# The units of a state-space scan in another order, without the two spare products with zero in each

## The chip, the cores and the metric

The kernel runs on one NeuronCore of one Trainium2 chip. The metric is the device time of one launch in microseconds (us); a time is the median of the runs named beside it. The engines are called by the names of the profile: PE (TensorE; PEld are its weight loads), DVE (VectorE), ACT (ScalarE), POOL (GpSimd) and SP (SyncE, which only issues DMAs here).

## What is computed

A small network on an image of 2 x 16 x 16 positions with 64 channels: an edge attention, an attention with rotary positions, a second attention, a mixture of experts, six layers of a state-space model, and a second mixture of experts. The change is in the state-space layers only. For each of the six layers and both batches (256 positions, 128 inner channels, 16 states):

```python
residual = hidden + residual
hidden = rmsnorm(residual, norm_w[i])
u, z = split(hidden @ in_w)                       # 128 channels each
uc = silu(causal_conv(u, cw) + cb)                # four taps
dt_r, Bm, Cm = split(uc @ xp_w)                   # 16 columns each
dt = softplus(dt_r @ dt_w + dt_b)
A = -exp(A_log)
h = exp(dt[..., None] * A) * h + (dt * u)[..., None] * Bm[:, None, :]   # along the positions
y = einsum('bds,bs->bd', h, Cm) + uc * D
hidden = (y * silu(z)) @ out_w
```

## The kernel before

The state-space layers run as 12 **units**, one for each layer and batch, `u = 0..11` with batch `b = u % 2`. In a unit the inner channels lie on the 128 partitions and the positions along the free axis. The 16 states are four **groups** `g` of four states `s`, so one operation of a group works on 128 x 1024 values. The order of work on each engine is written out by hand; engines wait for each other by semaphores, and each engine takes its instructions in the order in which they stand.

In a unit the work goes like this:

- ACT makes the decay factors, `decay` (L1487): one exponential of 128 x 255 for each state, 16 in a unit, four to a group.
- `drive` makes dt·u·B for a group: DVE for groups 0 and 1 (L1173), from rows of B that PE spreads over the partitions (`replicate`, L661, four small products; `spread_first`, `spread_second`), POOL for groups 2 and 3 (L1691), from rows that a DMA has spread.
- DVE scans each group along the positions (`scan`, L1182).
- `weigh` multiplies the states by C: POOL for groups 0 to 2 (L1702), the third in two halves; DVE for group 3 (`weigh_last`, L1192, two halves) from rows that PE spreads (`spread_last`).
- PE adds the 16 products up in PSUM by products with the identity (`sum_y` L694, `sum_third` L700, `sum_last` L708) on top of the product with D (`sum_skip`, L686).
- DVE multiplies the sum by silu(z) (`gate`, L1166), PE projects it and adds the residual (`out_proj`, L717 and L720).

Beside the scans of unit u, the next unit u+1 is prepared, and its input is the residual that unit u-1 of the same batch has just left: the squares (`prep_norm`, ACT, L1417), the root on POOL (`prep_rms`, L1674 and L1676), the scaled rows (`prep_hs`, ACT, L1431), turned by PE (`prep_transpose`, L622 to L626), copied (`prep_ht`, ACT, L1437), the convolution and the products for z (`prep_in`, PE, L633 to L637), tanh (`prep_tu`, ACT, L1443), `prep_uc` (DVE, L1148), `prep_x` (PE, L644 to L646: dt, B and C), the copies of B and C (`prep_xd`, ACT, L1461 and L1462), two steps that split them into three bf16 parts (`take_away` on PE, L653, and `prep_part` on ACT, L1467), the softplus (`prep_softplus`, ACT, L1471 to L1477), and `prep_dt` (DVE, L1154 to L1160).

Two products with a weight of zero, `idle_turns(2)` (L726), stand on PE between `sum_skip` and `prep_transpose` in each unit but the last; they add nothing to the sum. On PE a unit stands like this before the change:

```python
if u:
    sum_last(u - 1)
    sum_third(u - 1, 1).then_inc(sem("m_y"), 1)
    out_proj(u - 1)
spread_second(u); sum_skip(u); idle_turns(2); prep_transpose(u + 1); spread_last(u)
prep_in(u + 1); prep_x(u + 1); sum_y(u, 0); take_away(u + 1, 0)
sum_y(u, 1); take_away(u + 1, 1); sum_third(u, 0); spread_first(u + 1)
```

The functions that the change touches, with the line numbers of the profile:

Of the kernel before, what the change touches and what calls it, by code (L numbers as in the profile page):

```python
# [29 lines left out]
SG = 4  # L30
NSG = DS // SG
UNITS = NL * B
# [35 lines left out]
def hybrid(nc, x, const, w0, w1, w2, w3, w5, wm, rows, out):  # L68
    ctx = ExitStack()
    with ctx:  # L70
# [7 lines left out]
        def sem(name):  # L78
            if name not in sems:
                sems[name] = ctx.enter_context(nc.semaphore(name))  # L80
            return sems[name]
# [25 lines left out]
        ident = CONST.of(cst, "ident")  # L107
# [170 lines left out]
        def _(pe):  # L278
# [350 lines left out]
            def prep_in(u):  # L629

                i, b = divmod(u, 2)
                pe.wait_ge(sem("m_ht"), u + 1)
                pe.matmul(ups, bias[:, :, 0], pick_b[:, i:i + 1].to_broadcast([96, N]), start=True, stop=False)  # L633
                pe.matmul(ups, wcv[:, i, 0], ht[b][:, 3:3 + N], start=False, stop=False)
                pe.matmul(ups, wcv[:, i, 1], ht[b][:, 1:1 + N], start=False, stop=True).then_inc(sem("m_in"), 1)

                pe.matmul(zps, inz[:, i], ht[b][0:64, 3:3 + N], start=(u == 0), stop=True, skip_group_check=True)\  # L637
                    .then_inc(sem("m_in"), 1)

# [31 lines left out]
            def spread_second(u):  # L671

                pe.wait_ge(sem("m_dbu"), 2 * u + 1)
                replicate(u, SG)
# [10 lines left out]
                pe.wait_ge(sem("m_zs"), u + 1)  # L685
                pe.matmul(yps, dmat[:, i], uc[b], start=True, stop=True)  # L686

            def sum_y(u, g, zs_of=None):

                pe.wait_ge(sem("m_hc"), 4 * u + g + 1)  # L690
                if zs_of is not None:
                    pe.wait_ge(sem("m_zs"), zs_of + 1)
                for s in range(SG):
                    pe.matmul(yps, ident, hc[:, g, s], start=False, stop=True, skip_group_check=True)  # L694

            def sum_third(u, h):

                pe.wait_ge(sem("m_hc"), 4 * u + 3 + h)
                for s in range(2 * h, 2 * h + 2):
                    last = pe.matmul(yps, ident, hc[:, 2, s], start=False, stop=True, skip_group_check=True)  # L700
                return last

            def sum_last(u):

                for h in range(2):
                    pe.wait_ge(sem("m_hc3"), 2 * u + h + 1)
                    for s in range(2 * h, 2 * h + 2):
                        pe.matmul(yps, ident, hc[:, NSG - 1, s], start=False, stop=True, skip_group_check=True)  # L708

            def out_proj(u):  # L710

# [17 lines left out]
            def keep_awake(count, bank=5):  # L729

                for _ in range(count):
                    pe.matmul(PS[:, bank, N:2 * N], ident, CONST.of(cst, "rope")[:, 0:N], start=True, stop=True)  # L732
# [4 lines left out]
            keep_awake(1)  # L737
            pe.wait_ge(sem("m_weights"), 5)
            prep_in(0)
            keep_awake(3)  # L740
            prep_x(0)
            take_away(0, 0)
# [4 lines left out]
            for u in range(UNITS):  # L747
                more = u + 1 < UNITS
                if u:
                    sum_last(u - 1)  # L750
                    sum_third(u - 1, 1).then_inc(sem("m_y"), 1)
                    out_proj(u - 1)
                spread_second(u)
                sum_skip(u)
                if more:
                    idle_turns(2)
                    prep_transpose(u + 1)
                spread_last(u)
                if more:
                    prep_in(u + 1)  # L760
                    prep_x(u + 1)
                sum_y(u, 0, u + 1 if more else None)
                if more:
                    take_away(u + 1, 0)
                sum_y(u, 1)
                if more:
                    take_away(u + 1, 1)
                sum_third(u, 0)
                if more:
                    spread_first(u + 1)  # L770
            sum_last(UNITS - 1)
            sum_third(UNITS - 1, 1).then_inc(sem("m_y"), 1)
            out_proj(UNITS - 1)
            spare(1, 5)

# [38 lines left out]
        def _(v):  # L814
# [361 lines left out]
            def scan(u, g):  # L1176

                v.wait_ge(sem("m_dbu" if g < 2 else "m_dbu_pool"), 2 * u + g % 2 + 1)
                v.wait_ge(sem("m_da"), u * NSG + g + 1)
                if u and g < NSG - 1:  # L1180
                    v.wait_ge(sem("m_hc"), 4 * (u - 1) + (g + 1 if g < 2 else 4))
                v.tensor_tensor_scan(flat(hst[:, g]), flat(da[g % 2]), flat(dbu[:, g]),  # L1182
                                     0.0, ALU.mult, ALU.add).then_inc(sem("m_h"), 1)

# [109 lines left out]
        def _(act):  # L1294
# [174 lines left out]
            def prep_softplus(u):  # L1469

                act.activation(sp_a, dtp, ACT.Abs).then_inc(sem("m_sp"), 1)  # L1471
                act.wait_ge(sem("m_sp"), 4 * u + 1)
                act.activation(sp_v, sp_a, ACT.Tanh, scale=LOG_K, bias=turn_t).then_inc(sem("m_sp"), 1)
                act.activation(sp_u, sp_a, ACT.Exp, scale=-1.0, bias=logs_t).then_inc(sem("m_sp"), 1)
                prep_part(u, 1)
                act.wait_ge(sem("m_sp"), 4 * u + 2)
                act.activation(sp_w, sp_v, ACT.Tanh, scale=LOG_M, bias=shift_t).then_inc(sem("m_sp"), 1)  # L1477

# [25 lines left out]
            for u in range(UNITS):  # L1504
                more = u + 1 < UNITS
                decay(u, 0, every)
                decay(u, 1, every[0:3])
                if u:
                    act.wait_ge(sem("m_hid"), u)
                if u and more:  # L1510
                    prep_norm(u + 1)
                if u:
                    keep_residual(u - 1)
                decay(u, 1, every[3:4])
                if u and more:
                    prep_hs(u + 1)
                decay(u, 2, every[0:1])
                if more:
                    prep_ht(u + 1)
                decay(u, 2, every[1:3])  # L1520
                if more:
                    prep_tu(u + 1)
                decay(u, 2, every[3:4])
                if more:
                    prep_zs(u + 1)
                decay(u, 3, every[0:2])
                if more:
                    prep_xd(u + 1)
                decay(u, 3, every[2:4])
                if more:  # L1530
                    prep_softplus(u + 1)
                    prep_z(u + 1)
                    prep_part(u + 1, 2)
# [32 lines left out]
        def _(pool):  # L1566
# [140 lines left out]
            for u in range(UNITS):  # L1707
                more = u + 1 < UNITS
                drive(u, 2)
                if u and more:  # L1710
                    prep_rms(u + 1)
                weigh(u, 0)
                drive(u, 3)
                weigh(u, 1)
                weigh(u, 2, 2)
                if more:
                    prep_gz(u + 1)
# [101 lines left out]
```

## Time and profile before

| what | value |
|---|---|
| median of 3 runs | 383.85 us (383.53 to 384.74) |
| the profiled execution, its own time | 383.59 us |
| span of the profiled execution | 381.8 us |
| mean granted clock of PE over the span | 0.939 of full speed |
| PE busy | 329.2 us (86%) |
| DVE busy | 285.5 us (75%) |
| ACT busy | 236.2 us (62%) |
| POOL busy | 195.9 us (51%) |
| the 12 units | from about 158 to 357 us of the span |

A row of the timeline gives start, duration, engine, line, operation, what is written from what, and in square brackets how long the engine had been idle before it and what ended that. A row of the chain gives start, duration and name of one piece of the chain of work that ended last. A row of the windows gives a stretch, its length, the busy time of PE, PEld, DVE, ACT and POOL in it with the number of instructions, the granted clock of PE (1.00 is 2.4 GHz, 0.50 is 1.2 GHz) and the DMA share.

### The profile page before, as it was taken

How to read it: one execution, taken by the hardware profiler on the slowest of the kernel's cores; microseconds unless marked ns; L12 is line 12 of the kernel's file. 1: busy time of each engine (PE TensorE's matmuls, PEld its weight loads, DVE VectorE, ACT ScalarE, POOL GpSimd, SP SyncE). 2: the span in 40 equal slices, each digit the busy share in tenths (PEclk: the TensorE clock that was granted, in tenths of full speed). 3: DMA queues.
4: the chain of work that ended last, by engine and by line, in shares of the span. 5: the costliest groups of instructions: out<-in, count | busy, mean ns of one | idle time of the engine just before them, and what ended most of it. 6: DMA issues, size and time to landing. Idle time of an engine off the chain costs nothing.

```text
span 381.8 us, 5717 instructions
## 1 busy us (share of the span) xinstructions
PE 329.2 (86%) x1904; PEld 233.6 (61%) x1904; DVE 285.5 (75%) x496; ACT 236.2 (62%) x674; POOL 195.9 (51%) x175
## 2 busy tenths in 40 slices
PE   4866998899989999689989889898898989878684
PEld 3354875556548547466667666676766767656562
DVE  2674477989764543599998989889898998988363
ACT  1103278887870664786877867777686877863163
POOL 2989200000000410397887968888696887967000
PEclk9995699999996899999999999999999999995968
DMA  7960400000000030635427163461725527160000
GB/s 212 364 119 3 124 2 1 2 2 1 3 0 2 5 108 0 212 127 218 169 110 274 33 250 113 164 231 51 278 67 211 162 116 278 34 245 0 1 2 14
DMA packets 19751, 41.07 MB, mean 108 GB/s; under 512 B 7986, under 2 KB 10626, under 8 KB 19594
## 3 DMA queue, kind: packets, MB, share of 16 engines
q1 hardware_dynamic: 19434, 40.38, 31.0%
q8 instruction: 15, 0.25, 0.3%
q10 hardware_dynamic: 288, 0.33, 0.3%
q14 instruction: 14, 0.11, 0.1%
HBM read 40.31 MB, written 0.39 MB: 107 GB/s over the span
## 4 chain that ended last, share of the span: by engine, by line
PE 52%; DVE 28%; ACT 9%; issue 6%; POOL 3%; DMA 1%; DVEq 0%; SPq 0%; POOLq 0%; ACTq 0%
DVE big L1182 14%; PE PS L708 5%; PE PS L521 4%; DVE big L1192 3%; PE PS L661 3%; PE PS L700 3%; PE PS L297 2%; PE PS L485 2%; ACT PS L1487 2%; PE PS L415 2%; PE PS L732 2%; PE PS L585 2%; PE PS L291 2%; PE PS L495 2%; PE PS L622 2%
## 5 line engine op out<-in xcount | busy, mean ns | idle before, releaser
L1182 DVE TENSOR_TENSOR_SCAN big<-PS,big 128x1024 f32<-128x1024 f32 x48 | 109.6, 2287 | 5.6 <-ACT PS L1487 5.2
L1487 ACT ACTIVATE PS<-unit_t,amat 128x255 f32<-128x255 f32 x192 | 82.5, 467 | 20.7 <-DVE unit_t L1157 16.6
L1702 POOL TENSOR_TENSOR big<-big 128x1024 f32<-128x1024 f32 (+1 forms) x48 | 86.2, 1821 | 3.1 <-DVE big L1182 2.4
L1691 POOL TENSOR_TENSOR big<-unit_t,big 128x1024 f32<-128x1024 f32 x24 | 57.1, 2381 | 17.9 <-DMA big<-spill 17.9
L694 PE MATMUL PS<-big,cst 128*128 128x256 f32 x192 | 50.1, 407 | 1.3 <-POOL big L1702 1.2
L1658 POOL TENSOR_TENSOR w2t<-w2t,w0t 128x768 f32<-128x768 f32 x2 | 3.6, 1821 | 88.8 <-DVE big L1116 88.8
L694 PEld LDWEIGHTS PS<-big,cst 128*128 128x128 f32 x192 | 37.6, 201 | 8.1 <-POOL big L1702 2.6
L1298 ACT ACTIVATE big<-PS 128x512 f32<-128x512 f32 (+1 forms) x43 | 24.7, 583 | 22.5 <-PE PS L521 7.4
L1350 ACT ACTIVATE big<-PS,big 128x256 f32<-128x256 f32 x64 | 29.7, 474 | 1.5 <-DVE big L956 1.4
L1173 DVE TENSOR_TENSOR big<-unit_t,PS 128x1024 f32<-128x1024 f32 x24 | 29.0, 1208 | 1.7 <-PE PS L661 0.6
L661 PE MATMUL PS<-stack,pick_b 96*128 96x256 bf16 x144 | 22.2, 277 | 7.5 <-DVE big L1173 4.0
L956 DVE TENSOR_REDUCE big<-PS 128x2 f32<-128x512 f32 x32 | 22.0, 688 | 6.3 <-PE PS L485 3.0
L700 PE MATMUL PS<-big,cst 128*128 128x256 f32 x96 | 24.8, 380 | 0.0
L521 PE MATMUL PS<-cst,big 128*128 128x128 f32 x128 | 20.9, 285 | 3.2 <-ACT big L1298 1.9
L708 PE MATMUL PS<-big,cst 128*128 128x256 f32 x96 | 22.7, 379 | 0.0
L521 PEld LDWEIGHTS PS<-cst,big 128*128 128x128 f32 x128 | 13.5, 140 | 14.4 <-DVE big L965 6.9
L661 PEld LDWEIGHTS PS<-stack,pick_b 96*128 96x128 bf16 x144 | 12.5, 102 | 15.4 <-ACT stack L1467 7.6
L965 DVE TENSOR_SCALAR big<-big 128x256 f32<-128x256 f32 x64 | 19.7, 351 | 1.1
L700 PEld LDWEIGHTS PS<-big,cst 128*128 128x128 f32 x96 | 17.7, 193 | 3.1
L708 PEld LDWEIGHTS PS<-big,cst 128*128 128x128 f32 x96 | 17.3, 190 | 2.1
L1674 POOL TENSOR_TENSOR msq<-ssq,eps_t 128x2 f32<-128x2 f32 x11 | 2.2, 197 | 29.3 <-ACT sqs L1417 29.3
L1192 DVE TENSOR_TENSOR big<-big,PS 128x512 f32<-128x512 f32 x24 | 15.4, 684 | 0.4
(336 smaller groups left out, 663.2 us busy)
## 6 DMA issues: line engine op xcount, KB each, us to landing
big<-spill SPq DMA_DIRECT2D x60, 512.0 KB, 5.9
w3t<-in_w SPq DMA_DIRECT2D x1, 1588.0 KB, 13.6
big<-routed SPq DMA_DIRECT2D x8, 128.0 KB, 2.9
w2t<-in_w SPq DMA_DIRECT2D x1, 896.0 KB, 9.8
cst<-in_const SPq DMA_DIRECT2D x1, 848.0 KB, 7.7
w5t<-in_w SPq DMA_DIRECT2D x1, 812.0 KB, 6.0
w2t<-in_wm SPq DMA_DIRECT2D x1, 768.0 KB, 4.7
w1t<-in_w SPq DMA_DIRECT2D x1, 385.0 KB, 8.2
```

What stands on the lines that cost most here:

```text
L521: last = pe.transpose(PS[:, 6 + t, m * N + a * P:m * N + (a + 1) * P], probs[:, i % SLOTS, a, m * P:(m + 1) * P], ident)
L661: last = pe.matmul(PS[:, 4 + c, s * N:(s + 1) * N], pick_b[:, col:col + 1].to_broadcast([96, P]), stack[u % 2][:], start=True, stop=True)
L694: pe.matmul(yps, ident, hc[:, g, s], start=False, stop=True, skip_group_check=True)
L700: last = pe.matmul(yps, ident, hc[:, 2, s], start=False, stop=True, skip_group_check=True)
L708: pe.matmul(yps, ident, hc[:, NSG - 1, s], start=False, stop=True, skip_group_check=True)
L1173: v.tensor_tensor(dbu[:, g], dtu[u % 2].unsqueeze(1).to_broadcast([P, SG, N]), BCv, ALU.mult)\
L1182: v.tensor_tensor_scan(flat(hst[:, g]), flat(da[g % 2]), flat(dbu[:, g]), 0.0, ALU.mult, ALU.add).then_inc(sem("m_h"), 1)
L1192: v.tensor_tensor(hc[:, g, s], hst[:, g, s], BCv[:, s], ALU.mult).then_inc(sem("m_hc3"), 1)
L1350: act.activation(probs[:, i % SLOTS, a], PS[:, i % 4, a * N:(a + 1) * N], ACT.Exp, bias=rowmax[:, i, a:a + 1], accum_out=rowsum[:, i, a:a ...
L1487: one = act.activation(da[g % 2][:, n, 1:N], dt[u % 2][:, 1:N], ACT.Exp, scale=amat[:, u // 2, col:col + 1])
L1691: pool.tensor_tensor(dbu[:, g], dtu[b].unsqueeze(1).to_broadcast([P, SG, N]), bsp[b][:, SG * (g - 2):SG * (g - 1)], ALU.mult).then_inc(sem ...
L1702: pool.tensor_tensor(hc[:, g, s:s + size], hst[:, g, s:s + size], csp[u % 2][:, SG * g + s:SG * g + s + size], ALU.mult).then_inc(sem("m_h ...
```

## The change

Within each unit the order on PE, ACT and POOL changes, and the products with zero are no longer issued (the function stays, nothing calls it). No operation is added; `weigh` for groups 0 and 1 is cut into two halves like that for group 2, and each sum on PE waits for the half that it reads. `prep_in` is cut in two, so that the product for z stands behind `spread_last`.

```diff
+            def prep_in_z(u):
+
+                i, b = divmod(u, 2)
                 pe.matmul(zps, inz[:, i], ht[b][0:64, 3:3 + N], start=(u == 0), stop=True, skip_group_check=True)\
...
+            def sum_y(u, g, some):
+
+                for s in some:
+                    if g < NSG - 1:
+                        pe.wait_ge(sem("m_hc"), 6 * u + 2 * g + s // 2 + 1)
+                    else:
+                        pe.wait_ge(sem("m_hc3"), 2 * u + s // 2 + 1)
+                    last = pe.matmul(yps, ident, hc[:, g, s], start=False, stop=True, skip_group_check=True)
                 return last
...
                 if u:
-                    sum_last(u - 1)
-                    sum_third(u - 1, 1).then_inc(sem("m_y"), 1)
                     out_proj(u - 1)
+                sum_skip(u)
                 spread_second(u)
-                sum_skip(u)
                 if more:
-                    idle_turns(2)
                     prep_transpose(u + 1)
+                sum_y(u, 0, (0,))
+                if more:
+                    prep_in(u + 1)
                 spread_last(u)
                 if more:
-                    prep_in(u + 1)
+                    prep_in_z(u + 1)
                     prep_x(u + 1)
-                sum_y(u, 0, u + 1 if more else None)
+                    pe.wait_ge(sem("m_zs"), u + 2)
+                sum_y(u, 0, (1, 2, 3))
+                sum_y(u, 1, (0,))
                 if more:
                     take_away(u + 1, 0)
-                sum_y(u, 1)
+                sum_y(u, 1, (1, 2, 3))
                 if more:
                     take_away(u + 1, 1)
-                sum_third(u, 0)
+                sum_y(u, 2, (0, 1))
+                sum_y(u, 3, (0,))
+                sum_y(u, 2, (2,))
                 if more:
                     spread_first(u + 1)
...
+                sum_y(u, 2, (3,))
+                sum_y(u, 3, (1, 2, 3)).then_inc(sem("m_y"), 1)
             out_proj(UNITS - 1)
...
                 act.activation(sp_a, dtp, ACT.Abs).then_inc(sem("m_sp"), 1)
+                prep_part(u, 1)
                 act.wait_ge(sem("m_sp"), 4 * u + 1)
...
-                prep_part(u, 1)
...
-                weigh(u, 0)
+                weigh(u, 0, 2)
                 drive(u, 3)
-                weigh(u, 1)
+                weigh(u, 1, 2)
                 weigh(u, 2, 2)
```

On ACT the 16 decays lie otherwise between the preparing steps; the two places below show the engines that wait there.

On PE, around the turned rows, from the projection of the unit before (L717, L720) to the convolution. In the kernel before, L661 is a spread, L686 the product with D, L726 the products with zero, L622 to L626 the turned rows:

```order
L717 MATMUL PS<-Y,cst 128x128
L720 MATMUL PS<-wout,unit_t 128x64 x2
L661 MATMUL PS<-stack,pick_b 128x256 x4
L686 MATMUL PS<-unit_t,w0t 128x256
L726 MATMUL PS<-cst,zero_t 128x256 x2
L622 MATMUL PS<-cst,hs 64x128
L624 MATMUL PS<-moved,hs 64x129
```

and after the change, where L708 and L711 are the projection, L689 the product with D, L664 a spread and L698 a sum with the identity:

```order
L708 MATMUL PS<-Y,cst 128x128
L711 MATMUL PS<-wout,unit_t 128x64 x2
L689 MATMUL PS<-unit_t,w0t 128x256
L664 MATMUL PS<-stack,pick_b 128x256 x4
L622 MATMUL PS<-cst,hs 64x128
L624 MATMUL PS<-moved,hs 64x129
L622 MATMUL PS<-cst,hs 64x128
L626 MATMUL PS<-cst,hs 64x127
L698 MATMUL PS<-big,cst 128x256
L633 MATMUL PS<-pick_b,bias 128x256
```

The products with zero are gone, the product with D stands ahead of the second spread, and one sum stands between the turned rows and the convolution, where a spread stood.

On PE at the end of a unit, from the second `take_away` to the projection. Before:

```order
L653 MATMUL PS<-stack,less 96x256
L700 MATMUL PS<-big,cst 128x256 x2
L661 MATMUL PS<-stack,pick_b 128x256 x4
L708 MATMUL PS<-big,cst 128x256 x4
L700 MATMUL PS<-big,cst 128x256 x2
```

and after:

```order
L656 MATMUL PS<-stack,less 96x256
L698 MATMUL PS<-big,cst 128x256 x4
L664 MATMUL PS<-stack,pick_b 128x256 x4
L698 MATMUL PS<-big,cst 128x256 x4
L708 MATMUL PS<-Y,cst 128x128
```

Two of the six sums that stood behind the first spread of the next unit stand ahead of it now.

On ACT, from tanh to the split of B and C; L1487 and L1483 are the decays, L1443 and L1439 tanh, L1461, L1462 and L1457, L1458 the copies of B and C. Before:

```order
L1443 ACTIVATE unit_t<-PS 128x256
L1487 ACTIVATE PS<-unit_t,amat 128x255
L1448 ACTIVATE unit_t<-PS 128x256
L1487 ACTIVATE PS<-unit_t,amat 128x255 x2
L1461 ACTIVATE xds<-PS 96x256
L1462 ACTIVATE stack<-PS 96x256
L1487 ACTIVATE PS<-unit_t,amat 128x255 x2
L1471 ACTIVATE big<-PS 128x256
```

and after:

```order
L1439 ACTIVATE unit_t<-PS 128x256
L1483 ACTIVATE PS<-unit_t,amat 128x255
L1444 ACTIVATE unit_t<-PS 128x256
L1483 ACTIVATE PS<-unit_t,amat 128x255 x2
L1457 ACTIVATE xds<-PS 96x256
L1458 ACTIVATE stack<-PS 96x256
L1483 ACTIVATE PS<-unit_t,amat 128x255
L1467 ACTIVATE big<-PS 128x256
```

The decay behind tanh was the last of group 2 and is the first of group 3 now; one decay of group 3 is left behind the copies, where there were two.

## Rows read from the trace of the kernel before

**Rows 1.** The windows: one unit, gate to gate (columns: see above).
```profile
257.52:273.86 16.34, 14.73 (x78) 10.99 (x78) 14.72 (x15) 12.24 (x36) 13.71 (x10) 1.00 0.46 166
```

**Rows 2.** The timeline of DVE over one unit, gate to gate.
```profile
273.52 0.42 DVE L1166 TENSOR_TENSOR unit_t<-PS,unit_t 128x256 f32<-128x256 f32 x1 [0.80 <-PE PS L700]
...
282.87 2.29 DVE L1182 TENSOR_TENSOR_SCAN big<-PS,big 128x1024 f32<-128x1024 f32 x1 [0.46 <-ACT PS L1487]
285.19 1.29 DVE L1192 TENSOR_TENSOR big<-big,PS 128x512 f32<-128x512 f32 x2
...
287.84 1.22 DVE L1173 TENSOR_TENSOR big<-unit_t,PS 128x1024 f32<-128x1024 f32 x1
289.86 0.42 DVE L1166 TENSOR_TENSOR unit_t<-PS,unit_t 128x256 f32<-128x256 f32 x1 [0.80 <-PE PS L700]
```

**Rows 3.** The chain of waits over the same unit, in order of time.
```profile
278.09 0.28 PE PS L633
...
282.01 0.77 ACT PS L1487 x2
...
286.63 0.60 PE PS L661 x4
287.22 1.73 PE PS L708 x8
288.95 0.88 PE PS L700 x4
```

**Rows 4.** The timeline of POOL in that unit, and its halves by form.
```profile
276.27 2.36 POOL L1702 TENSOR_TENSOR big<-big 128x1024 f32<-128x1024 f32 x1
278.59 2.36 POOL L1691 TENSOR_TENSOR big<-unit_t,big 128x1024 f32<-128x1024 f32 x1
280.92 4.82 POOL L1702 TENSOR_TENSOR big<-big 128x1024 f32<-128x1024 f32 x3
...
L1702 POOL TENSOR_TENSOR big<-big 128x512 f32<-128x512 f32 x24 | 30.1, 1281 | 0.0
```

**Rows 5.** The timeline of PE from the second spread to the turned rows.
```profile
274.49 0.60 PE L661 MATMUL PS<-stack,pick_b 96*128 96x256 bf16 x4
274.93 0.60 PE L686 MATMUL PS<-unit_t,w0t 128*128 128x256 f32 x2
275.36 1.03 PE L726 MATMUL PS<-cst,zero_t 128*128 128x256 f32 x4
276.86 0.32 PE L622 MATMUL PS<-cst,hs 128*64 128x128 f32 x1 [0.47 <-ACT hs L1431]
...
277.24 0.27 PE L622 MATMUL PS<-cst,hs 128*64 128x128 f32 x1
```

**Rows 6.** The timeline of ACT: the last split of B and C in that unit.
```profile
285.47 0.38 ACT L1467 ACTIVATE stack<-PS 96x256 bf16<-96x256 f32 x1
```

**Rows 7.** The timeline of the first unit: PE, POOL, DVE.
```profile
159.72 0.61 PE L661 MATMUL PS<-stack,pick_b 96*128 96x256 bf16 x4 [1.32 <-DVE big L1173]
...
162.16 2.35 POOL L1702 TENSOR_TENSOR big<-big 128x1024 f32<-128x1024 f32 x1 [0.58 <-DMA big<-spill]
...
175.47 0.42 DVE L1166 TENSOR_TENSOR unit_t<-PS,unit_t 128x256 f32<-128x256 f32 x1 [0.66 <-PE PS L700]
```

**Rows 8.** The timeline of PE in the last unit, and its full-speed counterpart.
```profile
281.16 1.89 PE L694 MATMUL PS<-big,cst 128*128 128x256 f32 x8
...
342.67 1.04 PE L661 MATMUL PS<-stack,pick_b 96*128 96x256 bf16 x4 [1.78 <-DVE big L1173]
344.04 3.78 PE L694 MATMUL PS<-big,cst 128*128 128x256 f32 x8 [0.34 <-POOL big L1702]
```

**Rows 9.** The windows around PE's longest waits (clock: the third number from the end).
```profile
158.23:159.72 1.49, 0.17 (x3) 0.01 (x1) 1.25 (x2) 1.49 (x5) 0.53 (x1) 1.00 1.02 393
...
340.72:342.20 1.48, 0.17 (x1) 0.00 (x0) 1.48 (x2) 0.61 (x2) 0.57 (x1) 1.00 0.04 17
342.30:344.30 2.00, 1.30 (x5) 0.70 (x6) 1.97 (x2) 0.96 (x3) 2.00 (x2) 0.50 0.00 0
```

More of the change, by code:

```diff
@@ L686, in sum_skip @@
                 pe.matmul(yps, dmat[:, i], uc[b], start=True, stop=True)
[L688 to L700, printed above, removed]
-                return last
[L703 to L708, printed above, removed]
+            def sum_y(u, g, some):
[5 more added lines that the diff above has]
+                    last = pe.matmul(yps, ident, hc[:, g, s], start=False, stop=True, skip_group_check=True)
+                return last
             def out_proj(u):
@@ L739, in _ @@
             prep_in(0)
+            prep_in_z(0)
             keep_awake(3)
@@ L749, in _ @@
                 if u:
-                    sum_last(u - 1)
-                    sum_third(u - 1, 1).then_inc(sem("m_y"), 1)
                     out_proj(u - 1)
+                sum_skip(u)
                 spread_second(u)
-                sum_skip(u)
                 if more:
-                    idle_turns(2)
                     prep_transpose(u + 1)
+                sum_y(u, 0, (0,))
+                if more:
+                    prep_in(u + 1)
                 spread_last(u)
                 if more:
-                    prep_in(u + 1)
+                    prep_in_z(u + 1)
                     prep_x(u + 1)
-                sum_y(u, 0, u + 1 if more else None)
+                    pe.wait_ge(sem("m_zs"), u + 2)
+                sum_y(u, 0, (1, 2, 3))
+                sum_y(u, 1, (0,))
                 if more:
                     take_away(u + 1, 0)
-                sum_y(u, 1)
+                sum_y(u, 1, (1, 2, 3))
                 if more:
                     take_away(u + 1, 1)
-                sum_third(u, 0)
+                sum_y(u, 2, (0, 1))
+                sum_y(u, 3, (0,))
+                sum_y(u, 2, (2,))
                 if more:
                     spread_first(u + 1)
-            sum_last(UNITS - 1)
-            sum_third(UNITS - 1, 1).then_inc(sem("m_y"), 1)
+                sum_y(u, 2, (3,))
+                sum_y(u, 3, (1, 2, 3)).then_inc(sem("m_y"), 1)
             out_proj(UNITS - 1)
@@ L1180, in scan @@
                 if u and g < NSG - 1:
-                    v.wait_ge(sem("m_hc"), 4 * (u - 1) + (g + 1 if g < 2 else 4))
+                    v.wait_ge(sem("m_hc"), 6 * (u - 1) + 2 * g + 2)
                 v.tensor_tensor_scan(flat(hst[:, g]), flat(da[g % 2]), flat(dbu[:, g]),
@@ L1506, in _ @@
                 decay(u, 0, every)
-                decay(u, 1, every[0:3])
+                decay(u, 1, every[0:2])
                 if u:
@@ L1513, in _ @@
                     keep_residual(u - 1)
-                decay(u, 1, every[3:4])
+                decay(u, 1, every[2:3])
                 if u and more:
                     prep_hs(u + 1)
+                decay(u, 1, every[3:4])
                 decay(u, 2, every[0:1])
@@ L1519, in _ @@
                     prep_ht(u + 1)
-                decay(u, 2, every[1:3])
+                decay(u, 2, every[1:4])
                 if more:
                     prep_tu(u + 1)
-                decay(u, 2, every[3:4])
+                decay(u, 3, every[0:1])
                 if more:
                     prep_zs(u + 1)
-                decay(u, 3, every[0:2])
+                decay(u, 3, every[1:3])
                 if more:
                     prep_xd(u + 1)
-                decay(u, 3, every[2:4])
+                decay(u, 3, every[3:4])
                 if more:
```

## The prediction

> **What bounds it now.** Read the windows first: a unit takes 16.34 us, PE is busy for 14.73 of it and DVE for 14.72, at a granted clock of 1.00 [rows 1]. Neither is full, so the order of the work counts and not only its amount. The timeline of DVE shows where its time goes: it waits twice in a unit, 0.80 us for PE before the gate and 0.46 us for ACT before the fourth scan [rows 2]. The chain of waits says why [rows 3]. From the gate it runs over the first scan, the root on POOL, the turned rows, the convolution (278.09), the rest of the preparation of the next unit, the last two decays on ACT (282.01), the fourth scan and the two halves that DVE weighs; then PE spreads (286.63), adds six products (eight passes of L708 and four of L700, 2.61 us) and releases the next gate at 289.86. That is one loop through all four engines, once a unit. A change gains what it takes out of this loop, until another loop is as long.
>
> **The sums behind the first spread.** Today six sums stand between that spread and the gate; after the change four do. A sum is two passes, 1.73 us / 4 = 0.43 us [rows 3], so two of them are 0.87 us. DVE could take the gate as soon as its own product before it ends, 287.84 + 1.22 = 289.06, and not at 289.86 [rows 2]: the 0.80 us of idle time is the most that this edit can give.
>
> **The decays.** One decay instead of two stands between the copies of B and C and the fourth scan. Two cost 0.77 us in the chain [rows 3], so one is about 0.40, and the wait of 0.46 before the fourth scan [rows 2] shrinks to 0.06 or so. The moved decays of group 1 and 2 fill ACT's waits for PE and POOL; I cost them at nothing, covered by the wait for the turned rows. Without that cover each is 0.40 us. The earlier first split of B and C (`prep_part` ahead of the tanh) makes ACT wait for PE in front of the softplus, and the softplus has to be ready when DVE ends its weighing at 285.19 + 1.29; I take it as hidden, with little to spare.
>
> **The waits that are added.** The first sum now stands on PE ahead of the convolution and waits for POOL's first half: 276.27 + 1.28 = 277.55, and 0.43 for itself, 277.98, against 278.09 at which the convolution starts [rows 3, 4]. It is hidden by 0.1 us; if POOL were later, the convolution and all behind it would be later by as much. The spread for group 3 gets behind the convolution; it is wanted only by DVE's weighing, 7 us later. No DMA is moved: SP's transfers wait for the copy of B and C, which comes no later than now.
>
> **What is late next: POOL.** With both edits DVE's loop would be 16.34 - 0.80 - 0.40 = 15.14 us. But now the second half of group 2 is wanted ahead of the spread. POOL starts weighing 276.27 - 273.52 = 2.75 us after the gate and then has no wait [rows 2, 4]. Whole groups take 2.32 us start to start (276.27 to 278.59), the product between them 2.33; three pieces, one whole and two halves, take 4.82, so two halves take 2.50, and cutting costs 0.14 us a group (0.28 a unit for the two that are cut newly). The first half of group 2 is then there at 2.75 + 2.46 + 2.33 + 2.46 + 1.28 = 11.28 us after the gate. From there PE has four sums, the spread (0.44) and four sums: 8 x 0.43 + 0.44 = 3.88, with about 0.2 for the last pass's way to DVE. That is 15.4; with 0.05 for the handovers I take a unit of **15.45 us**, 0.9 less than now. Both ends of this: no loop shorter than DVE without idle time, 16.34 - 1.26 = 15.08 (12.6 us over ten units), and no gain if ACT or POOL turn out to be late everywhere.
>
> Ten intervals between gates gain 10 x 0.9 = 9.0 us; the first gate gains up to its own wait of 0.66 [rows 7]. Sum of the order alone: -9.7 us.
>
> **The products with zero.** They run from 275.36, four passes of 0.22 us (1.73 / 8), while PE waits for the scaled rows in any case (it still idles 0.47 us after them, released by ACT at 276.86) [rows 5]. Taking them out shortens no chain: worth 0 by themselves. What they do is keep PE occupied. Without them PE waits about 1.5 us there (from the end of the spread to 276.86), then has about 0.45 us of turned rows (276.86 to the last pair at 277.24, and its 0.1), about 0.35 of waiting for POOL's first half, one sum, and the convolution. No row of before shows that stretch, so I bound it. A wait of 1.32 us in the first unit left the clock at 1.00; a wait of 1.78 us in the last unit, after the same projection, spread and product with D, was followed by a granted clock of 0.50, the lower level of 1.2 GHz [rows 7, 8, 9]. The new wait lies between, nearer to the one that stayed up. And in the first unit the new order makes PE wait from about 160.6 (a spread of 0.44, as from 274.49 to 274.93, and the turned rows [rows 5]) until POOL's first half at 162.16 + 1.28 = 163.4 [rows 4, 7], 2.8 us: longer than the wait that was followed by the fall, so there I expect the clock to fall.
>
> The Trainium skill (TensorE: Matmul & The Clock Gate, "Why this matters for your kernels") asks that PE not stand idle between bursts for longer than a length that lies above both 1.50 and 1.78 us; by it the spare products are not needed and the order's 9.7 us would all be kept, 373.9 us. The 1.78 us wait speaks against it here.
>
> **The price of a fall.** At 0.50 eight passes take 3.78 us instead of 1.89 [rows 8]: everything doubles. If the clock falls in that wait, the turned rows (0.45), the first sum (0.43) and the convolution (four passes of 0.22 and a short one of 0.11, 0.97) [rows 3, 5] take up to 1.85 us more on the way to `prep_uc`; from 0.88 (only the first two) to 1.85, less about 0.35, by which PE's loop (15.45) is now longer than DVE's (15.1). So 0.5 to 1.5 us each, and more if the lower level lasts into the sums, which makes me take **1.2**, from the upper half.
>
> **The rivals.**
> *Clock stays up* in all units but the first: -9.7 + 1.2 = -8.5, 375.1 us. For it: 1.32 stayed up. The case of the page, with the first unit kept too, 373.9, has 0.05 of its chance. Against it: the stretch has little work on both sides of the wait.
> *Clock falls in every unit* (slower): the place is the wait between the second spread and the turned rows, 11 times. 11 x 1.2 = 13.2 against 9.7, so +3.5, 387.1 us. It decides from nine falls on (9.7 / 1.2 = 8.1). For it: the stretch from the gate to the convolution is thin, and 1.50 is not far from 1.78.
> *The loop does not get shorter*: the split of B and C comes late because PE puts a sum that waits for POOL ahead of it, and the softplus is late for DVE in place of the sums. Then the 0.80 returns as a wait before `prep_dt`; 383 to 384 us. Against it: a margin of 0.63 today (ACT's last split ends at 285.85, DVE's weighing at 286.48) [rows 2, 6].
> That the change does not do what it says can be left out: the order on PE shows it.
>
> **Forecast.** The clock falls in the first unit and in some three of the ten later ones, according to how thin the stretch happens to be: 4 x 1.2 = 4.8, and -9.7 + 4.8 = -4.9. From the profiled execution's own 383.59 (span 381.8 and 1.8 around it, 0.26 under the median of 383.85) that is **378.7 us**; its own range is 376.5 to 381.5.
>
> Chances: forecast 0.40, clock stays up 0.26, clock falls in every unit 0.26, loop not shorter 0.08. About 0.3% is what a measurement of this kernel can tell from no change. The first two are faster, together 0.66; of the rest 0.27 slower (the third, and a little of the fourth), 0.07 the same. The range reaches down to the second case with some more of DVE's wait gained, 374.5, and up to every unit falling, 387.0; cases of both signs are in it.
>
> **What would show it.** Right: gates 15.4 to 15.5 us apart where the clock is 1.00; DVE's wait before the gate down from 0.80 to 0.3 to 0.4 and PE without a wait from the first sum of group 2 to the gate; the wait before the fourth scan under 0.3; PE's wait for the turned rows near 1.5 us; a granted clock of 0.50 behind the first unit's wait, and in some later units, with the gate after it some 1.2 us late. Wrong: a clock of 1.00 in all units, or of 0.50 in each; gates 16.3 apart at full clock; a new wait before DVE's L1154 line, which would be the softplus or the split.

## The result, and the profile after

The changed kernel takes **386.62 us** (median of 20 runs, 382.91 to 389.54) against 383.38 us for the kernel before, measured beside it (20 runs, 381.1 to 386.25): a ratio of 1.0063, 95% interval 1.0033 to 1.0092. It is slower, by a little over half a percent. The forecast of 378.7 us had said faster; 386.62 is just inside the range, and next to the 387.1 us of the rival in which the clock falls in every unit. (Ratios, here and below, come from the executions within 1.5% of the fastest of their kernel, which leaves out the three longest of these 20, 388.71 to 389.54 us, and in the last experiment one of 529.09 us at a mean granted clock of 0.557; medians are of all.)

The 20 executions differ in the mean granted clock: those at 0.918 to 0.927 take 382.91 to 384.98 us, those at 0.905 to 0.910 take 386.52 to 389.54, and four lie between. The profiled execution took 383.3 us, with a span of 381.2 and a mean clock of 0.927, so what follows shows the change near its best.

The windows of the changed kernel, which answer to [rows 1, 9], cut the span at the start of the first unit's first scan (the last expectation below calls it the second), at its gate, and ten gates later; the fifth row is a piece of a later unit.

```profile
0.00:160.63 160.63, 139.51 (x909) 92.83 (x910) 98.03 (x282) 85.57 (x245) 37.87 (x73) 0.92 0.22 63
160.63:177.49 16.86, 14.08 (x68) 10.44 (x68) 14.49 (x13) 11.01 (x30) 13.54 (x10) 0.90 0.52 190
177.49:339.01 161.52, 144.23 (x742) 106.30 (x740) 149.33 (x131) 121.97 (x361) 137.52 (x111) 0.96 0.45 164
339.01:381.20 42.19, 27.36 (x146) 19.22 (x144) 26.27 (x72) 16.91 (x41) 10.90 (x8) 0.86 0.07 27
243.50:246.90 3.40, 3.40 (x15) 2.39 (x14) 2.52 (x2) 2.18 (x6) 3.40 (x3) 0.50 0.00 0
```

Before, the same four pieces were 159.69, 15.78, 163.41 (ten times 16.34, all at 1.00) and 42.92 us. So the ten intervals gained 1.89 us, the piece behind them 0.73; the first unit lost 1.08 and the piece ahead of the units, whose code is the same, 0.94. The mean clock of 0.96 in the ten intervals says why they gained so little: four of them hold a stretch at 0.50, the lower of the two levels, like the 3.40 us of the last row; such a drop is called a fall below. The gates are 15.61 to 15.66 us apart in the six units without such a stretch and 16.90 to 16.96 in the four with one.

The timeline of DVE, first a unit that kept its clock (gates at 208.74 and 224.38), then one that lost it (gates at 240.00 and 256.93), answers to [rows 2].

```profile
208.74 0.42 DVE L1162 TENSOR_TENSOR unit_t<-PS,unit_t 128x256 f32<-128x256 f32 x1
...
214.94 0.42 DVE L1144 SCALAR_TENSOR_TENSOR unit_t<-unit_t,PS 128x256 f32<-128x256 f32 x1 [0.16 <-ACT unit_t L1439]
...
217.79 2.29 DVE L1178 TENSOR_TENSOR_SCAN big<-PS,big 128x1024 f32<-128x1024 f32 x1 [0.23 <-ACT PS L1483]
220.12 1.28 DVE L1188 TENSOR_TENSOR big<-big,PS 128x512 f32<-128x512 f32 x2
221.32 0.90 DVE L1150 SCALAR_TENSOR_TENSOR big<-big 128x256 f32<-128x256 f32 x1
...
224.38 0.42 DVE L1162 TENSOR_TENSOR unit_t<-PS,unit_t 128x256 f32<-128x256 f32 x1
...
247.69 0.42 DVE L1144 SCALAR_TENSOR_TENSOR unit_t<-unit_t,PS 128x256 f32<-128x256 f32 x1 [1.63 <-ACT unit_t L1439]
...
254.06 0.61 DVE L1150 SCALAR_TENSOR_TENSOR big<-big 128x256 f32<-128x256 f32 x1
...
256.93 0.43 DVE L1162 TENSOR_TENSOR unit_t<-PS,unit_t 128x256 f32<-128x256 f32 x1
```

With the clock up, the wait of 0.80 before the gate is gone altogether and that of 0.46 before the fourth scan is down to 0.23. In the unit that lost the clock DVE waits 1.63 instead of 0.16 for the tanh that `prep_uc` needs: the delay reaches DVE there. Some of it comes back at L1150, which takes 0.61 there instead of 0.90.

The timeline of PE shows where the clock falls: the first unit, the same unit as above with its clock, and the one without. It answers to [rows 5, 7].

```profile
161.54 0.27 PE L626 MATMUL PS<-cst,hs 128*64 128x127 f32 x1
164.48 0.76 PE L698 MATMUL PS<-big,cst 128*128 128x256 f32 x2 [2.67 <-POOL big L1699]
165.03 0.42 PE L633 MATMUL PS<-pick_b,bias 96*128 96x256 bf16 x1
165.25 1.06 PE L634 MATMUL PS<-ht,w2t 128*128 128x256 f32 x2
...
210.19 0.60 PE L664 MATMUL PS<-stack,pick_b 96*128 96x256 bf16 x4
212.07 0.32 PE L622 MATMUL PS<-cst,hs 128*64 128x128 f32 x1 [1.28 <-ACT hs L1427]
...
212.82 0.70 PE L698 MATMUL PS<-big,cst 128*128 128x256 f32 x2
...
213.47 0.59 PE L634 MATMUL PS<-ht,w2t 128*128 128x256 f32 x2
...
241.46 0.60 PE L664 MATMUL PS<-stack,pick_b 96*128 96x256 bf16 x4
243.34 0.36 PE L622 MATMUL PS<-cst,hs 128*64 128x128 f32 x1 [1.28 <-ACT hs L1427]
...
243.50 0.41 PE L622 MATMUL PS<-cst,hs 128*64 128x128 f32 x1
...
244.28 1.22 PE L698 MATMUL PS<-big,cst 128*128 128x256 f32 x2
...
245.51 1.06 PE L634 MATMUL PS<-ht,w2t 128*128 128x256 f32 x2
```

The two later units have the same wait, 1.28 us, to the hundredth. One goes on at full speed (the convolution's two passes of L634 take 0.59); the other is at the lower level from 243.50, and the same rows take 1.06. The wait alone does not tell which of the two happens. The place is always the same, though: in this profile and in a second one of the same kernel (below), all ten falls in the ten intervals begin between 0.02 us before and 0.41 us after the start of the turned rows, so at the end of this wait.

### The profile page after: what moved, and what is told of

Same layout as the page of the kernel before. It is cut to its first block, busy times and chain, and to the rows that moved or that the text cites. A ratio compares the mean times of both kernels' runs of the same rounds, so it can differ in the third digit from the quotient of the medians.

```text
span 381.2 us, 5653 instructions
## 1 busy us (share of the span) xinstructions
PE 325.2 (85%) x1860; PEld 228.8 (60%) x1860; DVE 288.1 (76%) x496; ACT 235.4 (62%) x674; POOL 199.8 (52%) x199
## 4 chain that ended last, share of the span: by engine, by line
PE 48%; DVE 29%; ACT 12%; issue 5%; POOL 4%; DMA 1%; DVEq 0%; SPq 0%; POOLq 0%; ACTq 0%
DVE big L1178 14%; PE PS L698 7%; ACT PS L1483 5%; PE PS L521 4%; DVE big L1188 3%; POOL big L1699 2%; PE PS L297 2%; PE PS L485 2%; PE PS L640 2%; PE PS L415 2%; PE PS L664 2%; PE PS L585 2%; PE PS L634 2%; PE PS L495 2%; PE PS L291 2%
## 5 line engine op out<-in xcount | busy, mean ns | idle before, releaser
L698 PE MATMUL PS<-big,cst 128*128 128x256 f32 x384 | 100.7, 401 | 5.8 <-POOL big L1699 4.7
L1483 ACT ACTIVATE PS<-unit_t,amat 128x255 f32<-128x255 f32 x192 | 82.4, 467 | 19.9 <-DVE unit_t L1153 16.7
L1699 POOL TENSOR_TENSOR big<-big 128x512 f32<-128x512 f32 x72 | 89.7, 1271 | 3.9 <-DVE big L1178 1.6
L698 PEld LDWEIGHTS PS<-big,cst 128*128 128x128 f32 x384 | 70.1, 196 | 24.8 <-POOL big L1699 13.5
L664 PE MATMUL PS<-stack,pick_b 96*128 96x256 bf16 x144 | 22.7, 281 | 1.2 <-DVE big L1169 1.2
L622 PE MATMUL PS<-cst,hs 128*64 128x128 f32 x48 | 9.0, 316 | 12.8 <-ACT hs L1427 12.8
L664 PEld LDWEIGHTS PS<-stack,pick_b 96*128 96x128 bf16 x144 | 14.5, 102 | 8.8 <-DVE big L1169 1.6
L297 PE MATMUL PS<-cst 128*128 128x256 f32 x52 | 15.8, 442 | 0.3 <-ACT wdt L1294 0.3
L1188 DVE TENSOR_TENSOR big<-big,PS 128x512 f32<-128x512 f32 x24 | 15.4, 684 | 0.4
L622 PEld LDWEIGHTS PS<-cst,hs 128*64 128x64 f32 x48 | 5.5, 148 | 16.2 <-ACT hs L1427 15.6
L1144 DVE SCALAR_TENSOR_TENSOR unit_t<-unit_t,PS 128x256 f32<-128x256 f32 x12 | 5.1, 422 | 13.2 <-ACT unit_t L1439 13.0
## 6 DMA issues: line engine op xcount, KB each, us to landing
w2t<-in_w SPq DMA_DIRECT2D x1, 896.0 KB, 10.2
```

Of the source, the lines that this page charges most:

```text
L664: last = pe.matmul(PS[:, 4 + c, s * N:(s + 1) * N], pick_b[:, col:col + 1].to_broadcast([96, P]), stack[u % 2][:], start=True, stop=True)
L698: last = pe.matmul(yps, ident, hc[:, g, s], start=False, stop=True, skip_group_check=True)
L1188: v.tensor_tensor(hc[:, g, s], hst[:, g, s], BCv[:, s], ALU.mult).then_inc(sem("m_hc3"), 1)
L1483: one = act.activation(da[g % 2][:, n, 1:N], dt[u % 2][:, 1:N], ACT.Exp, scale=amat[:, u // 2, col:col + 1])
L1699: pool.tensor_tensor(hc[:, g, s:s + size], hst[:, g, s:s + size], csp[u % 2][:, SG * g + s:SG * g + s + size], ALU.mult).then_inc(sem("m_h ...
```

## The experiments

All edits but that of the second experiment are made to the changed kernel, and ratios are against the kernel before on the same chip. "Ten intervals" is the time from the first unit's gate to the gate ten units later, 163.41 us before.

**Two spare products put back.** The order stays, the products with zero return in front of the turned rows.

```diff
                 spread_second(u)
                 if more:
+                    idle_turns(2)
                     prep_transpose(u + 1)
```

> The new order with the two spare products put back between the second spread and the turned rows. Theory 1 (the order saves about 0.72 us a unit, and what takes it back are falls of TensorE's clock at 1.32 us each in the wait that the spare products filled): gates 15.6 us apart in all ten intervals, granted clock 1.00 in all of them, at most one fall in the first unit; 375.5 to 377.5 us. Theory 2 (the new order itself, with its sums that wait for POOL ahead of the convolution, lets the clock fall or costs time elsewhere, whether or not the spare products are there): 385 to 387 us, gates of 16.9 us among those of 15.6.

Measured: 377.46 us (374.14 to 378.35), ratio 0.9829 [0.9789, 0.9869]. Its windows for the first unit and the ten intervals:

```profile
159.48:174.76 15.28, 13.56 (x72) 10.07 (x72) 14.64 (x12) 10.98 (x30) 13.54 (x10) 1.00 0.59 206
174.76:331.11 156.35, 147.40 (x781) 108.86 (x780) 150.12 (x132) 122.37 (x362) 137.27 (x111) 1.00 0.48 171
```

and a row of PE in one of the ten units:

```profile
209.34 0.32 PE L622 MATMUL PS<-cst,hs 128*64 128x128 f32 x1 [0.41 <-ACT hs L1428]
```

The clock is at 1.00 throughout, and all intervals are 15.61 to 15.66 us, with 0.41 us left of the wait for the turned rows. PE does more work than without the products and is done sooner. So the order alone is worth 163.41 - 156.35 = 7.06 us over the ten intervals, and the missing products cost what the changed kernel lost: 161.52 - 156.35 = 5.17 us there and 16.86 - 15.28 = 1.58 us in the first unit.

**The old order without its spare products.** The kernel before with one line out:

```diff
-                    idle_turns(2)
                     prep_transpose(u + 1)
```

> The old order without the two spare products, nothing else. Theory 1: the wait for the turned rows grows from 0.47 to about 1.3 us; the clock falls in some of the units, where a gate comes later by up to 1 us; 385 to 391 us. Theory 2 (only the new order is thin enough for a fall): gates 16.34 us apart throughout, 383.4 us within 0.3%.

Measured: 391.56 us (388.69 to 393.74), just above the range of theory 1, ratio 1.0194 [1.0146, 1.0242]. Its windows ahead of the units, for the first unit and for the ten intervals:

```profile
0.00:163.65 163.65, 141.43 (x906) 93.26 (x906) 98.12 (x282) 86.13 (x246) 37.60 (x73) 0.90 0.21 62
163.65:180.63 16.98, 14.50 (x70) 10.56 (x70) 14.39 (x12) 11.45 (x31) 14.21 (x8) 0.90 0.58 214
180.63:348.26 167.63, 142.78 (x742) 105.27 (x740) 147.18 (x130) 122.34 (x361) 134.50 (x91) 0.97 0.44 158
```

and a row of PE in a unit that lost its clock:

```profile
249.35 0.47 PE L622 MATMUL PS<-cst,hs 128*64 128x128 f32 x1 [1.33 <-ACT hs L1430]
```

The wait for the turned rows is 1.33 or 1.34 us in all ten units. Seven of the ten intervals are 16.34 as before and three, with a stretch at 0.50, are 17.73 to 17.75; the first unit takes 1.20 us more. In this order too the products pay only through the clock. Not all of this profile's 9.3 us is theirs, though: 3.96 stand ahead of the units, where a stretch at 0.50 (75.3 to 82.1 us) came in code that is the same. The next experiment's profile has that stretch as well, with its spare products in place.

**Six more in the first unit's wait.**

```diff
                 if more:
+                    idle_turns(2)
                     prep_transpose(u + 1)
+                if u == 0:
+                    idle_turns(6)
                 sum_y(u, 0, (0,))
```

> As the run with the two spare products put back, and six more behind the turned rows of the first unit alone, which fill the wait of 2.7 us for POOL's first half there. Theory 1: no fall in the first unit, the first gate up to 1.3 us earlier than with two spare products alone; 374.5 to 376.5 us. Theory 2 (the first unit is late for another reason, its DMA or POOL): the same time as with two spare products alone.

Measured: 376.55 us (375.33 to 378.88), ratio 0.9815 [0.9772, 0.9858], the same as with two products alone. The first unit keeps its clock but takes 15.93 us, more than the 15.28 above: six products last longer than the wait for POOL, and the first sum, behind them, starts 4.66 us after DVE's first scan and not 3.76 (167.32 - 162.66 against 163.24 - 159.48). In the run with two products alone the first unit had kept its clock without them, with a wait of 1.72 us; so this run says little about what a fall costs there.

**POOL's product for the gate, moved.** With the two spare products back, `prep_gz` (POOL, L1679) goes from the end of a unit to behind the next unit's first `drive`.

```diff
                 drive(u, 2)
+                if u:
+                    prep_gz(u)
...
                 weigh(u, 2, 2)
-                if more:
-                    prep_gz(u + 1)
```

> As the run with the two spare products put back, and POOL's product of z and its sigmoid (0.73 us) moved from the end of a unit to behind its first product for the next unit, so that it no longer runs beside the first of the three small DVE operations that make dt. Theory A (that DVE operation takes 0.90 us instead of 0.42 because POOL works beside it): 0.42 to 0.45 us again, gates 15.2 to 15.4 us apart (POOL's root is later by about 0.25), 372 to 375 us. Theory B (it is longer for another reason, such as a wait for ACT that the profile counts as work): it stays at 0.90, gates 15.6 to 15.9 us apart, 376 to 380 us.

Measured: 376.76 us (373.43 to 377.25), ratio 0.9785 [0.9738, 0.9832]; ten intervals 155.29 us. Three timelines carry it, POOL of the changed kernel:

```profile
211.49 2.51 POOL L1699 TENSOR_TENSOR big<-big 128x512 f32<-128x512 f32 x2
213.95 2.38 POOL L1688 TENSOR_TENSOR big<-unit_t,big 128x1024 f32<-128x1024 f32 x1
216.29 4.96 POOL L1699 TENSOR_TENSOR big<-big 128x512 f32<-128x512 f32 x4
221.21 0.72 POOL L1679 TENSOR_TENSOR unit_t<-unit_t 128x256 f32<-128x256 f32 x1
```

DVE of this run:

```profile
220.44 0.42 DVE L1151 SCALAR_TENSOR_TENSOR big<-big 128x256 f32<-128x256 f32 x1
...
223.37 0.42 DVE L1163 TENSOR_TENSOR unit_t<-PS,unit_t 128x256 f32<-128x256 f32 x1 [0.27 <-PE PS L698]
```

and PE's weight loads of this run:

```profile
219.16 1.59 PEld L698 LDWEIGHTS PS<-big,cst 128*128 128x128 f32 x8 [0.35 <-POOL big L1700]
```

In the changed kernel POOL's L1679 starts at 221.21 and DVE's L1150, the first step of the softplus polynomial, at 221.32, where it takes 0.90 us; apart from that product it takes 0.42. That 0.48 us filled the place of the wait before the gate. With the product moved DVE's step is back at 0.42, as theory A had it, but the gates are 15.53 us apart and not 15.2 to 15.4: the wait before the gate is back, at 0.27, released by PE's sums, and PE's weights for the first sum of group 2 wait for POOL until 219.16, 11.31 us after the gate at 207.85. That is the loop over POOL and PE that the prediction had named, with its 11.28 us. Breaking the collision gains only 0.1 us a unit, because that loop is next.

**The changed kernel once more**, with no edit, to see how the number of falls differs.

> The changed kernel once more, unchanged, to see a second execution in a profile. Theory 1 (the number of falls differs between executions of the same program, and each costs about 1.3 us): the profile shows another number of gates that are 16.9 us apart, all others 15.6; the gates of ten intervals together follow from the count as 156 + 1.3 times the number of falls. Rival (the number belongs to the program; executions differ for another reason): again four falls in the ten intervals, and in the same units.

Measured: 387.1 us (383.69 to 389.19), ratio 1.0072 [1.0034, 1.011]. Windows for the first unit and the ten intervals:

```profile
158.45:176.48 18.03, 15.45 (x68) 11.45 (x68) 14.30 (x13) 11.46 (x31) 13.78 (x10) 0.81 0.51 177
176.48:340.60 164.12, 146.97 (x742) 108.64 (x740) 148.94 (x130) 121.64 (x360) 137.16 (x111) 0.94 0.44 161
```

Six of the ten units lose the clock here, as theory 1 expected, in runs of neighbours (the third to the sixth interval, the ninth and the tenth; in the first profile the fifth to the seventh, and the tenth). Four are 15.62 to 15.64 and six 16.91 to 16.95, 1.31 us more each. The instructions are the same, the count is not. The first unit's 18.03 is 2.75 more than with spare products: its stretch at 0.50 lasts 6.8 us here.

**One spare product** instead of two, `idle_turns(1)` in the same place.

> The new order with one spare product with zero instead of two. If half of the work that the two brought is enough: no interval over 15.7 us, 376 to 378 us as with two. If the stretch between gate and convolution must be filled further: some intervals of 16.9 us, 379 to 384 us.

Measured: 377.42 us (376.55 to 379.51), ratio 0.9845 [0.9797, 0.9893]; ten intervals 156.33 us, all at 1.00. PE in one of the ten units:

```profile
213.08 0.32 PE L622 MATMUL PS<-cst,hs 128*64 128x128 f32 x1 [0.84 <-ACT hs L1428]
```

With a wait of 0.84 us one product is enough in the ten units. The first unit lost the clock for 10.2 us and took 19.46.

**Two spare products behind the turned rows**, so that the wait stays as long as in the changed kernel and the stretch has as much work as with two products in front.

```diff
                     prep_transpose(u + 1)
+                    idle_turns(2)
                 sum_y(u, 0, (0,))
```

> The new order with two spare products, but behind the turned rows and not ahead of them: the wait of about 1.3 us for the turned rows stays as in the changed kernel, the work of the stretch around it is that of the run with the spare products in the wait. They push the first sum and the convolution back by about 0.6 us, so intervals without a fall are 16.0 to 16.3 us. Theory W (the length of the one wait decides, as the prediction took it): falls as in the changed kernel, some intervals of 17.3 us or more, 386 to 392 us. Theory S (the amount of work in the whole stretch decides, wherever the wait lies): no fall in the ten intervals, 380 to 384 us.

Measured: 385.09 us (382.22 to 389.75), ratio 1.0017 [0.9981, 1.0053]. The timeline of PE in a unit that kept its clock:

```profile
209.01 0.60 PE L664 MATMUL PS<-stack,pick_b 96*128 96x256 bf16 x4
210.89 0.32 PE L622 MATMUL PS<-cst,hs 128*64 128x128 f32 x1 [1.28 <-ACT hs L1428]
...
211.48 1.13 PE L717 MATMUL PS<-cst,zero_t 128*128 128x256 f32 x4
212.44 0.59 PE L698 MATMUL PS<-big,cst 128*128 128x256 f32 x2
```

The wait is 1.28 us as in the changed kernel, and one unit in ten loses the clock (17.71 us) where four and six did. So the length of that one wait does not decide alone, against theory W; but theory S, with no fall at all, did not come true either. This profile took 382.56 us, near the best of its 12 executions; their mean clocks are 0.922 to 0.945, against 0.905 to 0.927 in all 30 executions of the changed kernel, so products beside the wait do hold the clock up. How well they do it in the median execution no profile shows. Here they also stand on the path, between the turned rows and the first sum, and the other nine intervals are 16.17 or 16.18 us: the order's gain is spent on them.

**The old order on ACT**, with two spare products in front: the decays, and the last split of B and C (`prep_part`), stand again where they stood before. The decays, in part:

```diff
-                decay(u, 1, every[0:2])
+                decay(u, 1, every[0:3])
...
-                decay(u, 3, every[3:4])
+                decay(u, 3, every[2:4])
```

> The new order of PE and POOL with two spare products, but the old order on ACT (two decays behind the copies of B and C, three of group 1 ahead of the squares, the first split behind two steps of the softplus). By the chain the fourth scan is later by one decay, 0.40 us, so its wait goes from 0.23 to about 0.6 us and intervals from 15.63 to about 15.9 to 16.1; 380 to 382 us. Rival (the decays lie beside other work anyway and only the four sums matter): 15.6 us and 376 to 378 us.

Measured: 379.53 us (377.31 to 381.57), ratio 0.9893 [0.9835, 0.995]; ten intervals 158.60 us, 15.86 each, both just under what was expected. DVE, then POOL:

```profile
215.80 2.29 DVE L1179 TENSOR_TENSOR_SCAN big<-PS,big 128x1024 f32<-128x1024 f32 x1 [0.53 <-ACT PS L1484]
...
219.32 0.49 DVE L1151 SCALAR_TENSOR_TENSOR big<-big 128x256 f32<-128x256 f32 x1
```

```profile
218.80 0.73 POOL L1679 TENSOR_TENSOR unit_t<-unit_t 128x256 f32<-128x256 f32 x1
```

The wait before the fourth scan is 0.53 instead of 0.23, and DVE's step of the polynomial takes 0.49 to 0.52 instead of 0.86 to 0.92, where it starts 0.52 us behind POOL's product (219.32 and 218.80) and not 0.11. ACT's new order is worth 0.23 us a unit, a third of the order's gain; the edit does not part the decays from the split.

**All that helped together:** two spare products, the moved `prep_gz`, and three more products behind the first unit's turned rows.

```diff
+                    idle_turns(2)
                     prep_transpose(u + 1)
+                if u == 0:
+                    idle_turns(3)
...
+                if u:
+                    prep_gz(u)
```

> Two spare products stand again ahead of the turned rows, POOL's gz product stands behind the next unit's drive product, and the first unit alone has three more spare products behind its turned rows, where PE waits for POOL's first half (2.04 us in the run with the moved gz product, with a clock fall right behind it). If a clock fall in the first unit costs 1.6 to 2.8 us there: no fall in any unit, first unit's second scan to gate 15.2 to 15.6 us, ten intervals of 15.5 us, and the time 374 to 376 us. Rival, the first unit's fall is hidden or the spare products there delay its first sums as much as the fall did: first unit 16 us or more and the time as with the moved gz product alone, 376.8 us.

Measured: **372.67 us** (372.07 to 373.92 without the one long execution), ratio 0.9709 [0.9664, 0.9753], faster than both kernels and below the 374 to 376 expected. The windows of the first unit and the ten intervals, and then the timeline of PE in the first unit:

```profile
159.11:174.31 15.20, 14.98 (x78) 11.15 (x78) 14.30 (x13) 11.34 (x31) 13.24 (x9) 1.00 0.59 209
174.31:329.60 155.29, 147.38 (x782) 108.91 (x780) 146.28 (x130) 122.26 (x362) 137.22 (x111) 1.00 0.48 171
```

```profile
161.09 1.56 PE L717 MATMUL PS<-cst,zero_t 128*128 128x256 f32 x6
162.87 0.70 PE L698 MATMUL PS<-big,cst 128*128 128x256 f32 x2 [0.22 <-POOL big L1702]
```

Three products end 0.22 us ahead of POOL's half and delay nothing. The first unit takes 15.20 us against 17.09 in the run with the moved product alone, where a wait of 2.04 us was followed by a fall. That is 1.9 of the 4.7 us between the two profiles' spans (370.8 and 375.5); 2.2 lie behind the ten intervals and 0.6 ahead of the units, where the code is the same.

## Why the prediction was wrong

**The step that failed is the count of falls:** "the clock falls in the first unit and in some three of the ten later ones", interpolated between a wait of 1.32 us that kept the clock and one of 1.78 that lost it. That the clock would fall, where, and at what price in the later units held; the count came from the wrong quantity. All later units of the changed kernel have the same wait, 1.28 us, shorter than the one that had kept the clock, and some fall while others do not: four in one profile, six in the other. (The wait itself was put at about 1.5 us, counted from 275.36, where the products with zero start; the product with D in front of them ends only at 274.93 + 0.60 = 275.53, which leaves 1.33, and that is what the old order without them shows.) With the same wait and products behind it, one falls; with a wait of 0.84 or 0.41, none, in six profiles with ten intervals each. What PE does around the wait counts beside its length, and which unit falls differs from execution to execution; why one falls and the next does not stays open.

In us, with the run with two products as the measure: the falls were to cost 4.8 and cost 5.17 + 1.58 = 6.75 in the first profile and 7.77 + 2.75 = 10.52 in the second; the order was to give 9.7 and gives 7.6. So the falls took back nearly all of the order's gain in the first profile and more than all of it in the second. The median execution is 386.62 - 383.3 = 3.3 us above the first profiled one; at 1.31 a fall that would be two or three falls more than its four, an estimate, since no profile caught such an execution.

The Trainium skill (TensorE: Matmul & The Clock Gate, "Why this matters for your kernels") asks only that PE not stand idle for longer than a length that lies above both 1.50 and 1.78 us; by that the later units would have kept their clock, and the prediction had put the time at 373.9 us for the case that the first unit keeps it too. The trace disagrees: the clock fell behind waits of 1.28 us, and of 1.33 us in the old order.

**The price of a fall:** 1.2 predicted; 16.90 to 16.96 against 15.61 to 15.66 is about 1.3, and 1.4 in the old order. In the first unit it was larger: 16.86 and 18.03 against 15.28 with the clock up, 1.6 and 2.8.

**The products cost nothing by themselves:** right. Returned, they leave the wait for the turned rows (0.41 us of it remains) and every interval as it is in units that kept their clock.

**The order's gain** was put at 9.7 us, ten intervals of 15.45 and 0.66 at the first gate. With the clock up they are 15.63 and 0.50 (15.28 instead of 15.78): 7.1 + 0.5 = 7.6 us. Of the missing 0.18 a unit, 0.10 is DVE's polynomial step beside POOL's product, which the prediction did not count, and 0.08 is the loop over POOL and PE, sized at 15.45 and measured at 15.53 once the collision is taken away. The wait before the gate, predicted at 0.3 to 0.4, is 0 because of the collision and 0.27 without it. The wait before the fourth scan was to shrink by 0.40, to 0.06; it shrank by 0.23, to 0.23 (and by 0.30 from the 0.53 of the old order on ACT).

**The sum for the profiled execution**, span against span: the forecast was 4.9 us under 381.8, and the measured span is 0.6 under, 4.3 off. The ten intervals are 3.5 of that (1.9 for the order's gain, 1.6 for one fall more at a slightly higher price), the first unit 0.5, the piece ahead of the units 0.9, and the piece behind them gives back 0.7; but for rounding the pieces add up. In the median execution, at a mean clock of about 0.91 against 0.927 here, the falls weigh more.

**The rivals:** "clock stays up" is what the run with the products back shows, 377.46 where 375.1 was worked out, but not this kernel. "Clock falls in every unit" gave nearly the right time, 387.1, from eleven falls at 1.2 against a gain of 9.7; the profiles show fewer falls, a dearer first unit and a smaller gain, so its time came out nearly right by luck. With a gain of 7.6 and 1.3 a fall the change turns slower from six falls on, not nine. "The loop is not shorter" fell: no wait appears at the softplus or the split.

## What to carry to other kernels

Work on TensorE that computes nothing can still be holding the clock up; before taking it out, ask what the engine does in the microseconds on both sides of the wait that it fills, and price the loss for every repetition, not for a share guessed from one wait's length. Spare products belong inside a wait, with an end just before its release: here, in front of the turned rows, they were free and worth 9 us (386.62 against 377.46); behind them they left one fall in ten units of the profiled execution and ate the gain (385.09). And when an order has pulled the waits out of an engine, look at which other engine's operation now runs beside its small ones.

## What the runs showed of the hardware that was not expected

A DVE operation of 0.42 us took 0.86 to 0.92 when a POOL product of 0.72 us had started just ahead of it, and 0.42 or 0.43 in all twelve units with that product elsewhere. The Trainium skill (SBUF — State Buffer, "Who interferes with whom") says that a DVE instruction with two inputs in SBUF and a GpSimd instruction that reads SBUF exclude each other for the whole instruction, and that the later one waits. The trace agrees: both inputs of DVE's step lie in SBUF, it starts 0.11 us behind POOL's product (221.32 and 221.21), and it ends only after that product (222.22 and 221.93). Wherever the step started beside a product that was already running, it ended 0.28 or 0.29 us behind the end of that product, so only a part of its 0.42 us was held up: it took 0.90 us when it started 0.11 behind the product, 0.61 at 0.40 (units that lost the clock), 0.55 at 0.48 (the first unit of the kernel before) and 0.49 at 0.52.

The same program lost its clock in four of ten units in one execution and in six in another, and the times of its first 20 executions spread over 382.91 to 389.54 us, 1.7%. Stretches at 0.50 also came and went in the code ahead of the units, which no edit touched: at 144.5 to 147.9 in one profile of the changed kernel and not in the other (first scan at 160.63 against 158.45), and at 75.3 to 82.1 in two other runs (163.65 and 162.66). What decides among equal units was not found.
